# Order of the roundings on ACT and POOL, the norms' last step and the routing of a gated attention layer

## The reference

```
A (32 groups h of 8 rows): kv[i,j] = k_i * v_j (k = v = ctx); y = causal convolution of kv
   with ssm_kernel[h] along the 512 positions, + kv * D[h]; out_j = sum over i of y[i,j] * q_i
F (per column of 128 (row, batch) pairs here; 16 heads):
   x = silu(x_prev * w0 + x * w1); q = silu(x Wq); k = x Wk; v = x Wv; g = x Wg
   q, k rotated; logits = v . router (2 experts per head); scores = softmax(logits)
   onehot = argmax; q_exp = q * score_of_the_chosen / count_of_the_chosen_so_far; k_exp = k * onehot
   o = (tril(q_exp k_exp^T) * scale) v; o = norm over the head; out = (silu(g) * o) Wout
```

## Time and profile before

| | |
|---|---|
| median of 3 runs | 1188.63 us |
| the profiled execution | 1192.39 us, span 1190.6 |
| busy of the span | PE 1006.2 (85%), DVE 861.2 (72%), POOL 647.1 (54%), ACT 349.1 (29%) |
| chain that ended last | PE 51%, POOL 25%, issue 14%, ACT 6%, DVE 2% |
| mean granted clock of PE | 0.933 |
| PE waits for qn | 73.5 us in 32 waits |
| PE waits for qx | 30.0 us in 31 waits |
| PE waits for gate_sb | 24.9 us in 32 waits |

### The profile page before, as it was taken

The page is one execution under the profiler, slowest core; times in us unless marked ns, Lnnn a source line. Parts: engine busy times, 40 slices in busy tenths (PEclk is TensorE's granted clock), DMA queues, the critical chain, the costliest instruction groups (busy, mean ns, idle before and its releaser), DMA issues.

```text
span 1190.6 us, 19510 instructions
## 1 busy us (share of the span) xinstructions
PE 1006.2 (85%) x7168; PEld 838.2 (70%) x7168; DVE 861.2 (72%) x1560; ACT 349.1 (29%) x714; POOL 647.1 (54%) x613
## 2 busy tenths in 40 slices
PE   1778988988879987889988898888888888889974
PEld 1567777777767776777767777777776777777863
DVE  5768777777776786777767887677785787787652
ACT  2333333332322332232322323232332332233221
POOL 5566555556654556565546656356654456665220
PEclk9889999999999999999989999899999999999987
DMA  8110111110111110011110111110111110011000
GB/s 266 40 39 2 50 49 50 50 49 12 39 50 50 50 49 23 29 49 50 50 50 2 48 50 50 50 46 10 43 49 50 50 50 20 30 50 36 10 10 18
DMA packets 25983, 52.50 MB, mean 44 GB/s; under 512 B 2544, under 2 KB 3696, under 8 KB 25904
## 3 DMA queue, kind: packets, MB, share of 16 engines
q1 hardware_dynamic: 22304, 46.59, 13.9%
q10 hardware_dynamic: 3600, 4.72, 1.3%
HBM read 42.75 MB, written 8.55 MB: 43 GB/s over the span
## 4 chain that ended last, share of the span: by engine, by line
PE 51%; POOL 25%; issue 14%; ACT 6%; DVE 2%; DMA 1%; POOLq 0%; ACTq 0%; SPq 0%; DVEq 0%
PE bank L320 16%; PE bank L294 12%; PE bank L281 10%; POOL kv_low L614 7%; PE bank L270 7%; POOL rot_b L643 4%; POOL rot_a L646 4%; POOL kv L605 3%; POOL rot_a L638 3%; PE bank L338 3%; PE bank L352 3%; ACT kv_high L484 2%; ACT gate_sb L577 2%; POOL rstd L620 2%; ACT qx L473 1%
## 5 line engine op out<-in xcount | busy, mean ns | idle before, releaser
L614 POOL TENSOR_TENSOR kv_low<-kv,kv_high 128x576 fp32r<-128x576 f32 x128 | 182.1, 1444 | 359.8 <-ACT kv_high L484 359.8
L294 PE MATMUL bank<-kv_high,toep 128*128 128x512 f32 x640 | 230.0, 417 | 11.2 <-DVE z_terms L717 6.0
L605 POOL TENSOR_TENSOR kv<-kx 128x512 f32<-128x512 f32 x128 | 159.3, 1244 | 6.6 <-DMA const<-shape_consts 6.6
L484 ACT ACTIVATE kv_high<-kv 128x576 fp32r<-128x576 f32 x128 | 84.2, 683 | 265.1 <-POOL kv L608 265.1
L294 PEld LDWEIGHTS bank<-kv_high,toep 128*128 128x128 f32 x640 | 126.1, 197 | 43.6 <-DVE z_terms L717 11.4
L281 PE MATMUL bank<-const,z_terms 128*128 128x128 f32 x1024 | 128.2, 287 | 30.0 <-ACT qx L473 30.0
L281 PEld LDWEIGHTS bank<-const,z_terms 128*128 128x128 f32 x1024 | 120.8, 149 | 43.4 <-ACT qx L473 43.3
L320 PE MATMUL bank<-w_all_high,yT_high 128*128 128x512 f32 (+2 forms) x512 | 139.8, 401 | 1.4 <-DVE gated L818 1.4
L320 PE MATMUL bank<-w_all_low,yT_high 128*128 128x512 f32 (+2 forms) x512 | 132.4, 387 | 0.0
L294 PE MATMUL bank<-kv_low,toep 128*128 128x512 f32 x320 | 129.9, 406 | 0.0
L620 POOL TENSOR_TENSOR o_rstd<-o_ve,minus_half 128x16 f32<-128x16 f32 x32 | 93.1, 2911 | 47.9 <-DVE o_ve L775 47.9
(11 more groups left out here) (100 smaller groups left out, 1861.6 us busy)
## 6 DMA issues: line engine op xcount, KB each, us to landing
toep<-taps_dram SPq DMA_DIRECT2D x32, 512.0 KB, 6.6
kx<-in_ctx SPq DMA_DIRECT2D x32, 384.0 KB, 6.9
x_in<-in_x SPq DMA_DIRECT2D x32, 256.0 KB
out_x<-out_sb SPq DMA_DIRECT2D x32, 256.0 KB
w_all<-in_L_ffn_Wv ACTq DMA_DIRECT2D x1, 1024.0 KB, 12.5
w_all<-in_L_ffn_Wg ACTq DMA_DIRECT2D x1, 1024.0 KB, 11.4
w_out<-in_L_ffn_Wout ACTq DMA_DIRECT2D x1, 1024.0 KB, 17.4
router<-in_L_ffn_router_w ACTq DMA_DIRECT2D x1, 512.0 KB, 7.5
```

Of the source, the lines that this page charges most:

```text
L294: ins = nc.tensor.matmul(bank[lc % 2][:, :], toep[:, 1 - p, a, (lc - mc) * P:(lc - mc + 1) * P], kv_p[b][:, 1 - p, mc, 0:FULL], start=(mc ...
L484: eng.activation(kv_p[0][:, p, c, :], kv[:, c % 2, :], ACT.Copy).then_inc(kv_high[c], 1)
L605: eng.tensor_tensor(view(kv[:, c % 2, 0:FULL], [[ROW, NROT], [1, ROW]]), view(kx[:, p, c, 0:ROW], [[0, NROT], [1, ROW]]), view(kx[:, p, c, ...
L614: eng.tensor_tensor(kv_p[1][:, p, c, :], kv[:, c % 2, :], kv_p[0][:, p, c, :].bitcast(F32), ALU.subtract).then_inc(kv_ready[c], 1)
```

## The change

ACT rounds kv 0 right behind y_raw and kv 1 right behind oT, and kv 2 behind v_sb. It takes over the last step of both norms, as x * rstd - mean * rstd: nmr1 (or nmr2) = -mean * rstd by a Copy with a pointer scale, then qn (or z) by an Identity with pointer scale and bias; qn stands behind the routing activations, z behind gate_sb. It makes ad = |d| from PSUM, th = tanh(ad/2) and th1 = 1 + th. POOL does rstd1 ahead of o_rstd. DVE does norm 1's statistics ahead of multiply 2 and adds nmu = -mean for both norms; d_log, score, score1, cnt_a, cnt, qn and z leave it; sel and u read d from PSUM, ratio reads the count from PSUM. The matmul's matrix becomes rank (the causal one plus a diagonal of position + 1), so the matmul gives sum(u_m, m <= p) + (pos + 1) * u_p, the count of the chosen expert with u's sign. The kernel multiplies it with 1 / th1, where th1 is twice the chosen score; ratio is so half of what it was, up to its sign, and as only its square is used, eps_w takes 4 * EPS.

```diff
@@ PE
-                    nc.tensor.matmul(bank[6][:, 0:RH], causal, u[:, :], start=True, stop=True).then_inc(cnt_ps, 1)
+                    nc.tensor.matmul(bank[6][:, 0:RH], rank, u[:, :], start=True, stop=True).then_inc(cnt_ps, 1)
-                        eng.wait_ge(route_b, 3 * h + 1)
+                        eng.wait_ge(ratio_ready, h + 1)
@@ ACT
+                if pre:
+                    kv_round(p, 0, h + 2)
                 if tail:
                     eng.wait_ge(oT_ps, h)
                     ...
+                if pre:
+                    kv_round(p, 1, h + 2)
...
-                if pre:
-                    kv_round(p, 0, h + 2)
-                    kv_round(p, 1, h + 2)
...
-                    eng.wait_ge(d_ready, h + 1)
-                    if can_wait(h):
-                        eng.wait_ge(route_a, h)
-                    eng.activation(th[:, :], d_log[:, :], ACT.Tanh, scale=0.5).then_inc(th_ready, 1)
+                    if can_wait(h):
+                        eng.wait_ge(rth1_ready, h)
+                    eng.activation(ad[:, :], bank[6][:, DK:DK + RH], ACT.Abs).then_inc(ad_ready, 1)
+                    eng.wait_ge(ad_ready, h + 1)
+                    eng.activation(th[:, :], ad[:, :], ACT.Tanh, scale=0.5).then_inc(th_ready, 1)
+                    eng.wait_ge(th_ready, h + 1)
+                    eng.activation(th1[:, :], th[:, :], ACT.Copy, bias=1.0).then_inc(th1_ready, 1)
                 if pre:
-                    kv_round(p, 2, h + 2)
+                    eng.wait_ge(rstd1_ready, h + 3)
+                    eng.activation(nmr1[:, :], nmu1[:, :], ACT.Copy, scale=rstd1[:, 0:1]).then_inc(nmr1_ready, 1)
+                    if can_wait(h + 2):
+                        eng.wait_ge(qT_ps, h + 2)
+                    eng.wait_ge(nmr1_ready, h + 3)
+                    eng.activation(qn[:, :], x_in[:, p, :], ACT.Identity, scale=rstd1[:, 0:1], bias=nmr1[:, 0:1]
+                                   ).then_inc(qn_ready, 1)
                     eng.wait_ge(qT_ps, h + 3)
...
                     eng.activation(v_sb[:, :], bank[4][:, :], ACT.Copy).then_inc(v_copied, 1)
                 if pre:
+                    kv_round(p, 2, h + 2)
                     kv_round(p, 3, h + 2)
...
                     eng.activation(gate_sb[:, :], bank[5][:, :], ACT.Silu).then_inc(gate_ready, 1)
+                if front:
+                    eng.wait_ge(rstd2_ready, h + 2)
+                    eng.activation(nmr2[:, :], nmu2[:, :], ACT.Copy, scale=rstd2[:, 0:1]).then_inc(nmr2_ready, 1)
+                    ...
+                    eng.activation(z[:, :], x2[:, (q + 1) % 4, :], ACT.Identity, scale=rstd2[:, 0:1], bias=nmr2[:, 0:1]
+                                   ).then_inc(z_ready, 1)
@@ POOL
-                if tail:
-                    rsqrt(o_rstd, o_ve, RH, o_ve_ready, h, o_rstd_ready)
                 if pre:
                     rsqrt(rstd1, ve1, 1, ve1_ready, h + 3, rstd1_ready)
+                if tail:
+                    rsqrt(o_rstd, o_ve, RH, o_ve_ready, h, o_rstd_ready)
@@ DVE
+                if pre:
+
+                    eng.wait_ge(s_x[p], 16 * (t + 2))
+                    eng.bn_stats(stats1[:, :], x_in[:, p, :]).then_inc(bn1_done, 1)
+                    ...
+                    eng.tensor_scalar(nmu1[:, :], mv1[:, 0:1], -1.0, None, ALU.mult)
+                    eng.tensor_scalar(ve1[:, :], mv1[:, 1:2], EPS, None, ALU.add).then_inc(ve1_ready, 1)
                 if front:
                     multiply(p, 2, h + 1)
...
-                    eng.tensor_copy(d_log[:, :], bank[6][:, DK:DK + RH]).then_inc(d_ready, 1)
-                    ...
-                    eng.tensor_scalar(qn[:, :], x_in[:, p, :], mv1[:, 0:1], rstd1[:, 0:1], ALU.subtract, ALU.mult
-                                      ).then_inc(qn_ready, 1)
+                    d = view(bank[6][:, DK:DK + 1], [[0, 2], [1, RH]])
+                    eng.tensor_scalar(sel[:, :, :, 0], d, 0.0, None, ALU.is_le)
+                    eng.tensor_scalar(sel[:, :, :, 1], d, 0.0, None, ALU.is_gt)
+                    eng.tensor_scalar(u[:, :], bank[6][:, DK:DK + RH], 0.0, 0.5, ALU.is_gt, ALU.subtract).then_inc(u_ready, 1)
...
-                    (score, score1, rscore)
+                    eng.wait_ge(th1_ready, h + 1)
+                    eng.reciprocal(rth1[:, :], th1[:, :]).then_inc(rth1_ready, 1)
...
-                    (cnt_a, cnt, ratio)
+                    eng.tensor_tensor(ratio[:, :], rth1[:, :], bank[6][:, 0:RH], ALU.mult).then_inc(ratio_ready, 1)
+                    eng.wait_ge(ratio_ready, h + 1)
+                    eng.scalar_tensor_tensor(out=eps_w[:, :], in0=ratio[:, :], scalar=4 * EPS, in1=ratio[:, :],
                                              op0=ALU.mult, op1=ALU.mult).then_inc(eps_ready, 1)
...
+                    eng.tensor_scalar(nmu2[:, :], mv2[:, 0:1], -1.0, None, ALU.mult)
                     eng.tensor_scalar(ve2[:, :], mv2[:, 1:2], EPS, None, ALU.add).then_inc(ve2_ready, 1)
...
-                    eng.tensor_scalar(z[:, :], x2[:, (q + 1) % 4, :], mv2[:, 0:1], rstd2[:, 0:1], ALU.subtract, ALU.mult
-                                      ).then_inc(z_ready, 1)
```

More of the change, by code:

```diff
@@ L96, in flamingo_gated_layer @@
         rstd1 = sb("rstd1", 1)
+        nmu1 = sb("nmu1", 1)
+        nmr1 = sb("nmr1", 1)
         qn = sb("qn", L)
@@ L108, in flamingo_gated_layer @@
         rstd2 = sb("rstd2", 1)
+        nmu2 = sb("nmu2", 1)
+        nmr2 = sb("nmr2", 1)
         z = sb("z", L)
-        d_log = sb("d_log", RH)
+        ad = sb("ad", RH)
         u = sb("u", RH)
@@ L113, in flamingo_gated_layer @@
         th = sb("th", RH)
[L114 to L118, removed]
+        th1 = sb("th1", RH)
+        rth1 = sb("rth1", RH)
         ratio = sb("ratio", RH)
@@ L628, in step @@
                     kv_rest(p, 1, h + 2)
+                if pre:
+                    rsqrt(rstd1, ve1, 1, ve1_ready, h + 3, rstd1_ready)
                 if tail:
                     rsqrt(o_rstd, o_ve, RH, o_ve_ready, h, o_rstd_ready)
-                if pre:
-                    rsqrt(rstd1, ve1, 1, ve1_ready, h + 3, rstd1_ready)
                 if back:
@@ L766, in step @@
                                       ).then_inc(y_low, 1)
+                if pre:
+                    eng.wait_ge(s_x[p], 16 * (t + 2))
+                    eng.bn_stats(stats1[:, :], x_in[:, p, :]).then_inc(bn1_done, 1)
+                    eng.wait_ge(bn1_done, h + 3)
+                    eng.memset(held[:, :], 0.0)
+                    eng.bn_aggr(mv1[:, :], stats1[:, :]).then_inc(mv1_done, 1)
+                    eng.wait_ge(mv1_done, h + 3)
+                    if can_wait(h + 2):
+                        eng.wait_ge(qn_ready, h + 2)
+                    eng.tensor_scalar(nmu1[:, :], mv1[:, 0:1], -1.0, None, ALU.mult)
+                    eng.tensor_scalar(ve1[:, :], mv1[:, 1:2], EPS, None, ALU.add).then_inc(ve1_ready, 1)
                 if front:
@@ L778, in step @@
                     multiply_last(p, h + 1)
[L779 to L787, removed]
                 if back:
-                    eng.wait_ge(logit_ps, h + 1)
+                    eng.wait_ge(ad_ready, h + 1)
                     if can_wait(h):
-                        eng.wait_ge(th_ready, h)
                         eng.wait_ge(cnt_ps, h)
-                    eng.wait_ge(qk_copied, h + 1)
-                    eng.tensor_copy(d_log[:, :], bank[6][:, DK:DK + RH]).then_inc(d_ready, 1)
[L796 to L804, removed]
-                    eng.tensor_scalar(qn[:, :], x_in[:, p, :], mv1[:, 0:1], rstd1[:, 0:1], ALU.subtract, ALU.mult
-                                      ).then_inc(qn_ready, 1)
+                        eng.wait_ge(qke_ready, h)
+                    d = view(bank[6][:, DK:DK + 1], [[0, 2], [1, RH]])
+                    eng.tensor_scalar(sel[:, :, :, 0], d, 0.0, None, ALU.is_le)
+                    eng.tensor_scalar(sel[:, :, :, 1], d, 0.0, None, ALU.is_gt)
+                    eng.tensor_scalar(u[:, :], bank[6][:, DK:DK + RH], 0.0, 0.5, ALU.is_gt, ALU.subtract).then_inc(u_ready, 1)
                 if setup_step:
@@ L824, in step @@
                 if back:
-                    eng.wait_ge(th_ready, h + 1)
-                    eng.wait_ge(u_ready, h + 1)
-                    eng.tensor_tensor(score[:, :], th[:, :], u[:, :], ALU.mult).then_inc(route_a, 1)
-                    eng.wait_ge(route_a, h + 1)
-                    eng.tensor_scalar(score1[:, :], score[:, :], 0.5, None, ALU.add).then_inc(route_c, 1)
-                    eng.wait_ge(route_c, 2 * h + 1)
-                    eng.reciprocal(rscore[:, :], score1[:, :]).then_inc(route_c, 1)
+                    eng.wait_ge(th1_ready, h + 1)
+                    eng.reciprocal(rth1[:, :], th1[:, :]).then_inc(rth1_ready, 1)
                 if front:
@@ L836, in step @@
                     eng.wait_ge(cnt_ps, h + 1)
[L837 to L845 removed]
+                    eng.wait_ge(rth1_ready, h + 1)
```

(9 more changed lines are left out.)

36 lines of the change are left out of this document (13 added, 23 removed).

## The result

| kernel | median us | ratio to before, 95% interval | profiled execution, span |
|---|---|---|---|
| before | 1188.35 (4 runs) | | 1192.39, 1190.6 |
| changed | 1040.96 (1039.40 to 1042.78, 4 runs) | 0.8765 (0.8737 to 0.8793) | 1042.78, 1040.6 |

The change makes the kernel faster by 12.4%. In the profiled executions 149.6 us went; 128 were forecast. Times and ratios here are of fast runs alone: one run of the kernel with the split output projection (5200.27 us) and one of the kernel before (1916.93 us) were slow and are left out.

The account below looks back on a forecast made before the run. A chain of waits between engines, with no engine full, bounds the kernel. Step 34.16 to 30.1 us saves 117 us over 29 steps, with both ends 128; 1192.4 - 128 - 3.8 = 1060 us, range 1042 to 1118.

Parts of the forecast that it names:

- the floor of 29.77 us: PE's step if both stops (qn 1.90, qx 0.87) and 1.62 us of half speed go from 34.16 us.
- an allowance of 0.35 us: Added to PE's step: 0.15 us for V's wait, 0.2 us for terms that may come late.
- The bound and the mechanism: No engine full; a chain passes between engines, with kv_high and kv_low on it only by their place in ACT's and POOL's queues.
- Arrival 1: What V projection waits for (gated's first product, behind o_rstd): V starts at 667.35 instead of 669.45, a wait of 0.15 us.
- Arrivals 2 and 3: add_transposed starts at 670.2, not 674.61, as V ends; scores, behind ACT's wait for rstd2, keep slack of 0.9 to 1.7 us.
- qn's leaving DVE: On DVE, qn stood ahead of gated on the path; moving it to ACT was credited with 1.48 us of the gain.
- The start: Step 0: its 4.14 us stop with slow transposes goes, 7 us; ahead of it qn and z leave DVE, 2 us.
- the end: In the last two steps V waits less: 2 us.
- the first rival: Arrival 1 fails: V waits 1 to 2 us, step 31.3 to 33.3, total 1095 to 1153, likeliest 1110; chance 0.16.
- table load: Slower rival: Abs or Identity outside SiLU's and Tanh's table set, so ACT loads tables in the loop; 1200 us; chance 0.04.
- above some 1.5 us: Claim that a V wait longer than this drops PE to 1.2 GHz, costing 1.62 us more.
- a wait for a whole kv_low: On DVE, nmu1 and ve1 could pay up to 1.4 us, putting V at 668.6 and the step at 31.0 or more.

Follow-up runs that it names:

- the kernel with the split output projection: Changed kernel with PE doing the output projection's first pass (4 of 12 matmuls) ahead of the transposes of qke, which wait for gate_sb: 1012.85 us, ratio 0.8503.
- the kernel with all orders and none of the work: Kernel before plus the moves of ACT's roundings (kv 0, 1, 2), norm 1's statistics and rstd1, without changed norms' last step, routing or counts: 1042.20 us, 0.8774.
- the kernel with the early x_in: Changed kernel with SP issuing the next load of x_in ahead of the store of out_sb: 1038.78 us, ratio 0.8715.

## Why the prediction was right and where it was wrong

**The step that failed** is the size of the step: the floor of 29.77 us took each stop of PE at its idle time alone, and an allowance of 0.35 us was put on top of it for lateness. The runs show a step of 29.42 us where nothing holds V, and 0.07 us of lateness.

**The bound and the mechanism: right.** Both stops went, the clock rose to 1.00 in the ordinary step, kv_low 0 and 1 stand apart ahead of o_ve. That the kernel became PE's own chain, but for gate_sb, is shown by its chain of waits, and that the orders alone do it by the kernel with all orders and none of the work.

**Arrival 1: right, and narrow as said.** o_rstd ends 9.15 us after oT starts (610.15 and 601.00); 9.6 was forecast, so the sum of that path was 0.4 too long. The wait ahead of V was forecast at 0.15 and is about 0.1: V starts 0.47 behind the transposes of qn where it is 0.35 for gated's. x_in's landing: in the kernel with kv 0 and 1 undone DVE waits for it in 22 steps, and shows when it comes, with SP's issue of the same step:

```profile
615.43 0.64 SPq L248 DMA_DIRECT2D x_in<-in_x  x1
```

```profile
621.67 0.69 DVE L790 BATCH_NORM_STATS2 stats<-x_in 128x6 f32<-128x512 f32 x1 [0.44 <-DMA x_in<-in_x]
...
622.62 0.15 DVE L797 TENSOR_SCALAR nmu<-mv 128x1 f32<-128x1 f32 x1
```

6.2 us from issue to use, against the 6.6 that I took from toep. In the changed kernel the statistics start 6.23 us behind the issue as well (604.15 and 597.92), as yT_low ends, so the landing may be earlier there.

**Arrivals 2 and 3: right.** add_transposed starts as V ends. ACT does wait for rstd2 in each step, 0.38 us, and expand takes 2.22 us beside a product, as feared; neither reaches PE.

**What DVE's lighter work is worth: half right.** The forecast gave the routing nothing, and it was worth nothing that the runs can tell. It gave qn's leaving DVE 1.48 us of the gain. That was wrong: with rstd1 early, qn on DVE is done before o_rstd is. The credit belongs to the place of rstd1, and of the statistics that it needs: with both roundings moved and rstd1 late, PE still waits 0.4 us a step for qn on DVE, and with all orders it doesn't.

**The size: wrong by two terms of the step.** The step was forecast at 30.12, rounded to 30.1, and is 29.49 in the mean of the ordinary steps; 29 steps of 0.63 are 18.3 of the 22.0 us that were missing (the spans give 150.0 won, and 128 were forecast).
- The floor, 34.16 - 1.90 - 0.87 - 1.62 = 29.77, is too high by 0.35: the kernel with the early x_in has steps of 29.42 in the mean. I subtracted each stop as long as the trace shows it idle. But where there is no stop, a group also starts ahead of the last one's end. The transposes of qn start at 610.55, 0.15 ahead of the count matmul's end at 610.70. add_transposed starts at 613.89, 0.17 ahead of V's end at 614.06, and the next group starts 3.50 us behind it, where it was 3.55 behind a stop (644.00 and 640.45). Together these are 0.37. The split output projection shows the same in another place: 0.78 idle, 0.9 won. So the term was a stop's price: its idle time and another 0.1 to 0.2 us.
- The allowance of 0.15 and 0.2 for V's wait and for terms that come late: 0.07 was needed, 0.28 too much.

The rest is small. The last two steps of each trip cost 6.0 us more than ordinary ones before and 5.6 after, 2.4 us over five trips, where I had counted nothing. In three of the five a stop ahead of the attention output (L339; nothing that the profile shows ended it) is longer than before, 0.4 to 3.3 us where it was 0.2 to 0.5. The start (9.4 us won, 9 forecast) and the end (2.7 and 2) fit. 18.3 + 2.4 + 1.1 = 21.8, against 22.0.

**The range.** Its lower end supposed a step of 29.6, so it rested on the same floor. At its upper end, 1118 leaves out 35 of the 58 us of the first rival's span (1095 to 1153), and not a third; that did not matter here.

**The rivals.** No table load entered the loop: the changed kernel has two, 1283 ns each, as before. Here the Trainium skill, "ScalarE: Activation LUTs", section "Table sets: the hidden batching unit", held: Abs and Identity ran without one. The clock did not follow "above some 1.5 us": a stop of 1.90 us lowered it in every ordinary step of the kernel before, and in every second one with kv 2 moved alone.

For nmu1 and ve1 the prediction took a wait for a whole kv_low from the Trainium skill, "SBUF — State Buffer", section "Who interferes with whom". The Trainium skill has it there for a tensor_scalar only in a 2-port mode; whether one of 128x1 enters such a mode no run shows. The lines above, beside POOL's of the same kernel, show no such wait: nmu1 took 0.15 us at 622.62, inside two kv_low of 622.36 to 625.18.

```profile
622.36 2.82 POOL L634 TENSOR_TENSOR kv_low<-kv,kv_high 128x576 fp32r<-128x576 f32 x2 [9.55 <-ACT kv_high L485]
```

## What to carry to other kernels

When a chain of waits runs through an engine's work that its receiver doesn't need yet, the order of that queue is the first thing to change: here moving three roundings (kv 0 and 1, and kv 2) brought 127 of 147 us, and all orders together the whole. Waits in one chain cover each other, so the parts of such a change neither add up (11.7 and 61.1 alone, 127.1 together) nor cost alone what they show: undo each in the changed kernel too. Where a stop of PE goes, count its idle time, the overlap of its neighbours and the slow stretch behind it; and fill the last stop with a piece of work that waits for nothing.

## What the runs showed of the hardware

- A stop of PE costs more than its idle time even at full clock: 0.78 us idle, 0.9 us in the step; add_transposed 3.71 instead of 3.49 us behind a stop of 0.87.
- Stops of equal length don't lower the granted clock each time. With a stop of 1.90 us in every step and no other but gate_sb's it fell in every second (steps of 33.2 and 31.7 us, granted clock 0.78 and 1.00 around V). Behind 2.24 us the same 32 transposes took 5.2 to 5.4 us in 26 of 30 steps and 3.71 in four; behind some 4.5 us they took 5.05 to 6.67 in every step.
- A tensor_scalar of 128x1 on DVE isn't held up by POOL's tensor_tensor (0.15 us inside it), where a scalar_tensor_tensor of 128x16 with two SBUF inputs took 0.92 us beside one and 0.17 in POOL's idle time. qn's tensor_scalar of 128x512 took 0.54 us inside POOL's power o_rstd, and 1.48 beside a rotary product.
- The hold-up works both ways: expand (128x1024, two SBUF inputs) took 2.22 us in the changed kernel, where POOL had begun a product 0.08 us ahead of it. With all orders and none of the work it began together with POOL's product of 128x64 and took 1.21; that product took 1.39 us instead of 0.32.
